# A two-layer sequence model on one core: a new order of the instructions of all engines and a new table of PSUM banks

## The chip, the cores and the metric

The kernel runs on 1 core of one Trainium2 chip. The metric is the time of the device in microseconds (us). The engines are PE (TensorE), DVE (VectorE), ACT (ScalarE), POOL (GpSimd) and SP (SyncE); each takes its own instructions strictly in the order in which the program issues them, and they meet by semaphores.

## What is computed

32 sequences of 256 positions with 128 channels go through two layers. Each layer is an adaptive-norm block: attention or a recurrence, then a feed-forward net with FP4-rounded operands. All is in float32. Cut to what matters:

```python
def layer(x, mix, ffn, c, wmod):              # c: one condition per sequence
    sa, ca, ga, sb, cb, gb = silu(c) @ wmod    # shifts, scales, gates
    x = x + ga * mix(layernorm(x) * (1 + ca) + sa)
    return x + gb * ffn(layernorm(x) * (1 + cb) + sb)

def mix0(h):     # 32 heads of 4, linear attention with 2 decays per head
    q, k = rope(h @ Wq.T), rope(h @ Wk.T); v = h @ Wv.T
    S[t] = beta[t] * S[t-1] + phi(k[t]) v[t]   # phi = elu + 1; K[t] alike
    y = sum_m mix_m * (phi(q) S_m) / (phi(q) K_m + eps)
    return layernorm(h + y @ Wout.T + bout) * g + b

def mix1(h):     # RWKV: WKV recurrence over t (max-stabilised), channel mix
    k, v, r = (shifted mixes of layernorm(h)) @ (w_key, w_value, w_recept)
    x = h + wkv(decay, first, k, v) * sigmoid(r) @ w_output
    fk, fr = (shifted mixes of layernorm(x)) @ (f_w_key, f_w_recept)
    return x + sigmoid(fr) * (relu(fk) ** 2 @ f_w_value)

def ffn(h):      # blocks of 16 are scaled by max/6 and rounded to E2M1
    q = fp4(h); t = silu(q @ fp4(w_gate).T) * (q @ fp4(w_up).T)
    return fp4(t) @ fp4(w_down).T              # 128 -> 352 -> 128
```

## The kernel before

The work is cut into 16 pairs of sequences (512 tokens, 4 tiles of 128 rows). It is a software pipeline: in turn `n` the attention step of pair `n`, the feed-forward of layer 0 of pair `n - 1`, the recurrence of layer 1 of pair `n - 2` and the feed-forward of layer 1 of pair `n - 3` run side by side. `turns` issues turns 0 to 5, then a hardware loop over turns 6 to 15 (two to an iteration), then turns 16 to 19. Turns 0 to 2 and 17 to 19 are only partly filled.

What sets the order is written out by hand, engine by engine: each engine's `body(n)` is a list of steps `do(step, pair, part)`. The eight PSUM banks are given out by the table `BANK`; a step that writes a bank first waits, with `freed` (or `freed_at_ends`, which counts only in the turns outside the loop), for the step that read it last. So a new order or a new table brings new such waits.

The names used below; the first letter tells the stage: `a` layer 0's attention, `b` a feed-forward (of layer 0 or 1), `c` layer 1's recurrence and channel mix.

- `a1n`, `a1`: ACT normalizes the rows of the input (L515), PE turns them, ACT writes `hcol` of layer 0 in two halves (L660). `a2`: PE makes keys and queries (L940), DVE multiplies by the rotary table (`rope`, L1566, keys first), `a2r` adds (L1571).
- `a4`: DVE scans (L1591) and, in `a4m`, products `state` times `rope` of 128x1024 (L1617). `a5`: the shares of the two decays, on DVE (L1624 to L1631) and PE (L1009). `a3t`: ACT halves `mixp` (L690), which `a5` needs. `a5y`: ACT copies `ycol` (L695). `a6`: PE's z-matmuls from `ycol` and `hcolb` (L1021, L1022); `a1b` makes `hcolb` on ACT (L644). `a6s`, `a6n`: squares and normalization of z on ACT (`zn`, L550, L556), between them POOL's power. `a7`: `ucol`; `a8`: rows of it to `zn` (L532), which a DMA from POOL's queue adds to x.
- `b1v`, `b1n`: squares (L525) and normalization (L515) ahead of a feed-forward, with POOL's power between them. `b1c`: the affine to `hqcol` (L660). `b1R` on PE turns it back to rows (L1063); `b1m`, `b1q` on DVE scale and round (`xblk` L1427, `hq` L1440, L1441), with ACT's `b1` (`xmag`, L712) between them. `b3`: gate and up (L1125), `th` on ACT (L708), product on DVE (L1663). `b4`, `b4q`: the same scaling and rounding of `hid`, 128x1408 (L1427, L1440, L1441), with ACT's `hidcol` (L717) between. `b5`: PE turns `hid` in two halves (L1202), ACT copies them (L724, L726), `down` multiplies (L1236); `b6g` scales by the gate (`gcol`, L660). `b6c`: the rows out, of layer 0 into `xb` (L532), of layer 1 into `drow` (L621); a DMA from POOL's queue (L466) adds `drow` to `xb`, and `store` (L882, ACT's queue) waits for it.
- `c1v`, `c1n`, `c1`: as `a1n`, `a1`, for layer 1. `c1r`, `c2s`, `c2n`, `c2`: the inner layer norm of it (L1264, L550, `norm` L556, `xs` L731), POOL's power of b1 in the middle. `c3`: three shifted products for k, v, r (L1274, L1275). `c4a`: DVE's max-scan (`epst` L1690) and `wa` (L1696); `c4`: four `relu` on ACT (L748); `c4e`: two exponentials (L753); `c4b`, `c4s`, `c4v`, `c4n`, `c4p`: DVE's part (L1702 to L1723). `c4y`: `wy`. `c5`: L1297. `c5k`: `xk` (L1738). `c6`: fk (L1330), `relu` and square on ACT (L775, L779), eight steps. `c6b`: L1338. `c7`: DVE gates it (`fth`, L1744), PE adds it up (L1102); `c9`: ACT's `acol` (L660); `c8`: rows of it to `arow` (L532), which a DMA of POOL's queue (L461) adds to `xb`.

POOL takes powers (`rstd`, L425, L416, L433) of 128x4 numbers for all norms, in one fixed circle, and issues the three adding DMAs.

## Time and profile before

| what | us |
|---|---|
| median of 3 runs | 1453.92 |
| lowest, highest | 1448.10, 1456.07 |
| the profiled execution, its own time | 1457.73 |
| its span, first to last instruction | 1454.8 |

The profile is of one execution, on the slowest (here the only) core; the 2.9 us between its time and its span lie around the span. Busy times are sums over an engine's instructions; neighbours on one engine can overlap by some tenths of a us, so the step from one start to the next can be shorter than the duration. In the timelines a bracket behind an instruction tells how long its engine had stood idle and whose work let it go. The mean clock that TensorE was granted is 0.899 of full speed.

### The profile page before, as it was taken

What the parts mean: (1) busy time and instruction counts of PE and PEld (TensorE: products, weight loads), DVE (VectorE), ACT (ScalarE), POOL (GpSimd) and SP (SyncE); (2) the same over time, 40 slices, a digit from 0 to 9 for tenths busy, and PEclk for the clock granted to TensorE, in tenths of its full rate; (3) what the DMA queues carried; (4) which work ended last, traced back from release to release, by engine and by line L of the source; (5) the groups of instructions that cost most, each with busy time, mean ns of one, the idle gap of its engine ahead of it and who ended that gap; (6) DMA issues with size and microseconds to landing.
All of it is one profiled execution on the core that took longest, in us unless ns stands there. A gap on an engine that the chain in (4) does not pass through costs nothing.

```text
span 1454.8 us, 18749 instructions
## 1 busy us (share of the span) xinstructions
PE 1157.6 (80%) x5194; PEld 706.2 (49%) x5194; DVE 1134.4 (78%) x1637; ACT 1059.1 (73%) x2849; POOL 264.5 (18%) x382
## 2 busy tenths in 40 slices
PE   5375878989797888889897988889897979878653
PEld 3133444645455554646454555546464555546332
DVE  6758595969798897969797988969797979864613
ACT  4153857779696969777796969687877969677553
POOL 1001121021212111130213122211303121211000
PEclk9676988989899999989899989999899989989776
DMA  4000000010101010100101010101001010101010
GB/s 127 0 8 8 8 15 8 9 29 1 30 8 30 8 30 9 30 7 7 29 0 30 7 29 7 30 7 22 15 7 26 4 29 8 22 8 23 0 22 15
DMA packets 28360, 25.84 MB, mean 18 GB/s; under 512 B 2304, under 2 KB 21376, under 8 KB 28288
## 3 DMA queue, kind: packets, MB, share of 16 engines
q0 software_dynamic: 6912, 12.59, 5.0%
q1 hardware_dynamic: 12928, 8.29, 1.9%
...
q14 instruction: 50, 0.41, 0.1%
...
## 4 chain that ended last, share of the span: by engine, by line
DVE 26%; PE 23%; issue 22%; ACT 20%; POOL 6%; DMA 2%; ACTq 1%; SPq 0%; DVEq 0%; POOLq 0%
PE ps L923 4%; PE ps L1236 3%; DVE hid L1440 3%; ACT hq L525 2%; PE ps L1125 2%; DVE hid L1663 2%; DVE blk L1427 2%; DVE outer L1582 2%; DVE state L1591 2%; PE ps L1202 2%; PE ps L996 2%; DVE hid L1441 2%; ACT norm L515 2%; POOL rstd_of_f L425 2%; DVE hid L1433 2%
## 5 line engine op out<-in xcount | busy, mean ns | idle before, releaser
L1125 PE MATMUL ps<-wguT,hqcol 128*128 128x352 f32 x512 | 179.8, 483 | 17.7 <-ACT th L708 7.4
L1591 DVE TENSOR_TENSOR_SCAN state<-beta,outer 128x512 f32<-128x512 f32 x128 | 148.3, 1199 | 0.0
L1125 PEld LDWEIGHTS ps<-wguT,hqcol 128*128 128x128 f32 x512 | 93.8, 197 | 86.1 <-issue 25.1
L1440 DVE SCALAR_TENSOR_TENSOR hid<-hidcol,hid 128x1408 f32<-128x1408 f32 (+1 forms) x68 | 106.4, 1569 | 11.3 <-ACT hidcol L717 10.7
L923 PE MATMUL ps<-const,hq 128*128 128x128 f32 x128 | 37.8, 386 | 88.5 <-ACT hq L515 88.4
L1427 DVE TENSOR_REDUCE xblk<-ps 128x32 f32<-128x512 f32 x32 | 22.0, 687 | 100.2 <-PE ps L1063 100.2
L1236 PE MATMUL ps<-hidcol,wdT 128*128 128x256 f32 (+1 forms) x384 | 92.6, 392 | 0.0
L1663 DVE TENSOR_TENSOR hid<-th,ps 128x352 f32<-128x352 f32 x128 | 63.1, 514 | 25.6 <-PE ps L1125 17.3
L1236 PEld LDWEIGHTS ps<-hidcol,wdT 128*128 128x128 f32 (+1 forms) x384 | 73.8, 196 | 18.7 <-issue 6.7
L996 PE MATMUL ps<-state,const 128*32 128x512 f32 x256 | 74.0, 884 | 7.2 <-DVE state L1617 7.1
L1617 DVE TENSOR_TENSOR state<-state,rope 128x1024 f32<-128x1024 f32 x64 | 75.0, 1213 | 1.7
L923 PEld LDWEIGHTS ps<-const,hq 128*128 128x128 f32 x128 | 20.4, 163 | 114.9 <-issue 67.5
L923 PE MATMUL ps<-const,norm 128*128 128x128 f32 x256 | 65.5, 341 | 12.6 <-ACT norm L515 7.0
L708 ACT ACTIVATE th<-ps 128x352 f32<-128x352 f32 x128 | 57.8, 465 | 17.7 <-DVE hid L1663 9.0
L1202 PE MATMUL ps<-const,hid 128*128 128x128 f32 (+1 forms) x384 | 52.5, 290 | 21.7 <-DVE hid L1441 21.7
L1566 DVE TENSOR_TENSOR rope<-ps,const 128x1024 f32<-128x1024 f32 x32 | 38.8, 1212 | 39.0 <-PE ps L940 39.0
L717 ACT ACTIVATE hidcol<-hid 128x1408 f32<-128x1408 f32 x32 | 44.1, 1378 | 34.0 <-DVE hid L1433 34.0
L923 PEld LDWEIGHTS ps<-const,norm 128*128 128x128 f32 x256 | 37.1, 150 | 65.3 <-issue 36.6
L465 POOL TENSOR_TENSOR pool_scrap<-minus_half,eps_tile 128x4 f32<-128x4 f32 x16 | 7.4, 465 | 335.1 <-ACT drow L621 335.1
L1690 DVE TENSOR_TENSOR_SCAN epst<-neg_w,ps 128x256 f32<-128x256 f32 x32 | 20.2, 674 | 59.7 <-PE ps L1275 59.7
L940 PE MATMUL ps<-hcol,wqk 128*128 128x512 f32 x128 | 64.2, 631 | 1.3 <-ACT hcol L660 1.3
L1330 PE MATMUL ps<-xk,fw_key 128*128 128x512 f32 x128 | 63.8, 604 | 0.0
...
## 6 DMA issues: line engine op xcount, KB each, us to landing
...
```

The costliest lines, as they stand in the source:

```text
L708: s.activation(th[l][:, t % 2, :], bank(f"f{l}_g{t}")[:, 0:I_FF], ACT.Silu).then_inc(s_th[l], 1)
L923: last = t_.transpose(dst[:, t * P:(t + 1) * P], src[:, t, :], ident)
L940: ins = t_.matmul(two_banks(("a_k", "a_q")[h])[:, n_, :], wqk[:, k, :], hcol[0][:, :], start=True, stop=True)
L996: last = t_.matmul(bank("a_n")[c * NH:(c + 1) * NH, :], cst("sel_num"), state[:, m, c, :], start=(m == 0), stop=(m == M - 1), tile_positio ...
L1125: t_.matmul(bank(f"f{l}_{'gu'[g]}{t}")[:, 0:I_FF], hqcol[l][:, t * P:(t + 1) * P], wguT[:, l, g, :], start=True, stop=True).then_inc(s_gu[ ...
L1202: last = t_.transpose(bank(f"f{l}_h{k}{'aac'[c]}")[0:rn, col:col + P], hid[l][:, 2 * k + t, r0:r0 + rn], ident)
L1236: last = t_.matmul(bank(f"f{l}_d")[:, toks], wdT[0:rn, l, c, :], hidcol[l][0:rn, c, toks], start=(c == 0), stop=(c == 2))
L1330: t_.matmul(bank(f"c_f{c}"), fw_key[:, c * P:(c + 1) * P], xk[:, :], start=True, stop=True).then_inc(s_fk_mm, 1)
L1440: return v.scalar_tensor_tensor(dst, mag, low, dst, ALU.max, (ALU.add, ALU.subtract)[part])
L1591: return v.tensor_tensor_scan(state[:, m, c, :], beta[:, m, :], src, 0.0, ALU.mult, ALU.add)
L1617: v.tensor_tensor(state[:, m, 2 * h:2 * h + 2, :], state[:, m, 2 * h:2 * h + 2, :], qshare[:, m:m + 1, :].to_broadcast([P, 2, TOK]), ALU.m ...
L1663: v.tensor_tensor(hid[l][:, t, :], th[l][:, t % 2, :], bank(f"f{l}_u{t}")[:, 0:I_FF], ALU.mult).then_inc(s_hid[l], 1)
```

## The change

All steps and their instructions stay. New are the order of the steps on ACT, PE, DVE and POOL, the table `BANK`, and the waits for free banks that follow from both. The turn is also cut at another place: what stood at the end of a turn (`a4dp`, `b4q` of layer 0, `c7` on DVE; `c6`, `b5` of layer 1, `c6b`, `c7` on PE) now opens the next turn, with `n - 1` for `n`. POOL's circle of steps is the same, cut elsewhere. In SyncE nothing changes. Line numbers behind the table are lower by one.

```diff
-BANK = {"a_b0": 5, "a_b1": 0, "a_den": 6, "a_k": 3, "a_mix": 3, "a_n": 3, "a_nT": 3, "a_q": 1, "a_s0": 3,
+BANK = {"a_b0": 3, "a_b1": 7, "a_den": 2, "a_k": 3, "a_mix": 5, "a_n": 0, "a_nT": 2, "a_q": 1, "a_s0": 4,
...
@@ POOL
-                do(power_f0, n - 2)
-                do(power_c1, n - 3)
                 do(add_x4, n - 4)
...
                 do(add_x1, n - 1)
+                do(power_f0, n - 1)
+                do(power_c1, n - 2)
@@ ACT
-                do(c9, n - 3, 0)
-                do(c9, n - 3, 1)
+                do(a3m, n - 1)
+                do(c8, n - 3)
                 do(layer(b5, 0), n - 2, 0)
                 do(layer(b5, 0), n - 2, 1)
-                do(c8, n - 3)
+                do(store, n - 4)
                 do(a3t, n - 1)
-                do(store, n - 4)
                 do(layer(b6g, 0), n - 2, 0)
                 do(layer(b6g, 0), n - 2, 1)
+                do(layer(b1v, 1), n - 3)
                 do(layer(b6c, 0), n - 2)
-                do(layer(b1v, 1), n - 3)
+                do(a1b, n - 1)
                 do(c1v, n - 2)
                 do(layer(b1n, 1), n - 3)
+                do(layer(b1c, 1), n - 3, 0)
+                do(layer(b1c, 1), n - 3, 1)
                 do(c1n, n - 2)
...
+                do(c9, n - 2, 0)
+                do(c9, n - 2, 1)
                 do(layer(b6c, 1), n - 3)
@@ PE
             def a1(i):
-                freed(pe, s_yc, i - 1)
+                freed(pe, s_xs[0], i - 2)
+                freed_at_ends(pe, s_shch, i - 1, 2, 1)
                 turn(norm[0], bank("a_nT"), "a0", i)
...
             def body(n):
+                do(c6, n - 3, 2)
+                do(b5_1, n - 4, 0)
+                do(c6, n - 3, 3)
+                do(b5_1, n - 4, 1)
+                do(b5d_1, n - 4, 0)
+                do(a3m, n - 1)
+                do(c6b, n - 3)
+                do(b5d_1, n - 4, 1)
+                do(c7, n - 3)
+                do(b6r_1, n - 4)
+                do(a4d, n - 1)
+                do(c8, n - 3)
                 do(b5_0, n - 2, 0)
                 do(b5_0, n - 2, 1)
-                do(c8, n - 3)
                 do(b5d_0, n - 2, 0)
                 do(b5d_0, n - 2, 1)
                 do(b6x_0, n - 2)
+                do(a5, n - 1, 0)
                 do(b6r_0, n - 2)
-                do(a5, n - 1, 0)
                 do(a5, n - 1, 1)
...
@@ DVE
             def body(n):
+                do(a4dp, n - 1)
+                do(layer(b4q, 0), n - 2, 0)
+                do(c7, n - 3)
+                do(layer(b4q, 0), n - 2, 1)
+                do(layer(b4q, 0), n - 2, 2)
+                do(a4, n - 1, 0, 0)
...
-                do(layer(b4q, 0), n - 1, 1)
-                do(c7, n - 2)
-                do(layer(b4q, 0), n - 1, 2)
```

Three places of the loop follow as the built programs have them; rows for semaphores and registers are left out.

ACT from `mixp` of `a3t` to the normalization `c1n` of layer 1 (`gcol` is the gated `down` of layer 0, `xb` its rows, `hq` with `squares_f` is `b1v` of layer 1). Before:

```order
L690 ACTIVATE mixp<-mixp 128x256
...
L882 DMA out<-xb 128x4x128
...
L660 ACTIVATE gcol<-ps,mod_cols 128x256
...
L532 ACTIVATE xb,sums_a<-ps 128x128 x4
...
L525 ACTIVATE hq,squares_f<-xb,negm_f 128x128 x4
L525 ACTIVATE norm,squares_a<-xb,negm_a 128x128 x4
...
L515 ACTIVATE hq<-xb,shift_of_f,rstd_of_f 128x128 x4
...
L515 ACTIVATE norm<-xb,shift_of_a,rstd_of_a 128x128 x4
```

After:

```order
L882 DMA out<-xb 128x4x128
L690 ACTIVATE mixp<-mixp 128x256
...
L660 ACTIVATE gcol<-ps,mod_cols 128x256
...
L525 ACTIVATE hq,squares_f<-xb,negm_f 128x128 x4
...
L532 ACTIVATE xb,sums_a<-ps 128x128 x4
...
L644 ACTIVATE hcolb<-hcol,bout 128x512
L525 ACTIVATE norm,squares_a<-xb,negm_a 128x128 x4
...
L515 ACTIVATE hq<-xb,shift_of_f,rstd_of_f 128x128 x4
...
L660 ACTIVATE hqcol<-ps,mod_cols 128x256
...
L515 ACTIVATE norm<-xb,shift_of_a,rstd_of_a 128x128 x4
```

The squares of `b1v` now stand ahead of the rows `xb`, `hcolb` has come in, both halves of `hqcol` stand ahead of `c1n`, and the store ahead of `mixp`.

ACT from the squares of `c2s` to the first exponential of `c4e`. Before:

```order
L550 ACTIVATE norm,squares_b<-ps 128x128 x4
...
L556 ACTIVATE norm<-ps,rstd_of_b 128x128 x4
...
L695 ACTIVATE ycol<-ps 128x512
L731 ACTIVATE xs<-ps,vec 128x2x256
...
L515 ACTIVATE norm<-xa,shift_of_a,rstd_of_a 128x128 x4
...
L550 ACTIVATE zn,squares_z<-ps 128x128 x4
...
L712 ACTIVATE xmag<-hq 128x512
...
L748 ACTIVATE ex<-wa 128x512 x2
L748 ACTIVATE ex<-wa,less 128x512
L532 ACTIVATE zn,sums_f<-ps 128x128 x4
L824 ACT_TABLE_LOAD
...
L753 ACTIVATE ex<-ex 128x2x512
```

After:

```order
L550 ACTIVATE norm,squares_b<-ps 128x128 x4
...
L695 ACTIVATE ycol<-ps 128x512
L712 ACTIVATE xmag<-hq 128x512
L556 ACTIVATE norm<-ps,rstd_of_b 128x128 x4
...
L550 ACTIVATE zn,squares_z<-ps 128x128 x4
L731 ACTIVATE xs<-ps,vec 128x2x256
...
L515 ACTIVATE norm<-xa,shift_of_a,rstd_of_a 128x128 x4
...
L748 ACTIVATE ex<-wa 128x512
L532 ACTIVATE zn,sums_f<-ps 128x128 x4
L748 ACTIVATE ex<-wa 128x512
L823 ACT_TABLE_LOAD
...
L753 ACTIVATE ex<-ex 128x2x512
```

`ycol` and `xmag` have gone ahead of the normalization by `rstd_b`; the squares of z stand ahead of `xs`, and of the four `relu` (L748) two instead of three stand ahead of the exponential.

DVE from `wa` of `c4a` to `c4v`. Before:

```order
L1696 SCALAR_TENSOR_TENSOR wa<-epst,neg_w,ps 128x512
L1440 SCALAR_TENSOR_TENSOR hq<-xmag,hq 128x512
...
L1440 SCALAR_TENSOR_TENSOR hq<-xmag,hq 128x512
...
L1441 TENSOR_TENSOR hq<-hq,xblk 128x512
...
L1566 TENSOR_TENSOR rope<-ps,const 128x1024
L1571 TENSOR_TENSOR qk<-rope 128x512
L1546 SCALAR_TENSOR_TENSOR negm_f<-sums_f,negm_a 128x4
...
L1702 TENSOR_TENSOR ex<-ex,ps 128x512
L1709 SCALAR_TENSOR_TENSOR ab<-ex 128x512
...
L1566 TENSOR_TENSOR rope<-ps,const 128x1024
...
L1709 SCALAR_TENSOR_TENSOR ab<-ex 128x512
...
L1713 TENSOR_TENSOR ex<-ex,ps 128x512
```

After:

```order
L1695 SCALAR_TENSOR_TENSOR wa<-epst,neg_w,ps 128x512
...
L1565 TENSOR_TENSOR rope<-ps,const 128x1024
L1545 SCALAR_TENSOR_TENSOR negm_f<-sums_f,negm_a 128x4
L1570 TENSOR_TENSOR qk<-rope 128x512
...
L1565 TENSOR_TENSOR rope<-ps,const 128x1024
L1570 TENSOR_TENSOR qk<-rope 128x512
...
L1701 TENSOR_TENSOR ex<-ex,ps 128x512
L1708 SCALAR_TENSOR_TENSOR ab<-ex 128x512
...
L1708 SCALAR_TENSOR_TENSOR ab<-ex 128x512
...
L1712 TENSOR_TENSOR ex<-ex,ps 128x512
```

The rounding of `hq` (`b1q` of layer 1) has gone ahead of `wa`; both `rope` products and both sums `qk` now stand ahead of `c4b` (the first `ex`), where before one product and one sum did.

## Rows read from the trace of the kernel before

**Rows 1.** Page, part 1: busy us and share of the span, by engine.

```profile
PE 1157.6 (80%) x5194; PEld 706.2 (49%) x5194; DVE 1134.4 (78%) x1637; ACT 1059.1 (73%) x2849; POOL 264.5 (18%) x382
```

**Rows 2.** Busy time by stretch: stretch, length, PE, PEld, DVE, ACT, POOL, PEclk, DMA share, GB/s.

```profile
690.70:770.90 80.20, 69.68 (x325) 42.58 (x324) 69.00 (x98) 64.33 (x177) 16.17 (x23) 0.94 0.08 17
```

**Rows 3.** Chain that ended last, in order of time: start, us, engine and line.

```profile
289.99 2.80 PE ps L1236 x12
...
450.05 2.70 PE ps L1236 x12
...
1252.71 2.80 PE ps L1236 x12
```

**Rows 4.** Timeline of DVE, one turn: start, us, instruction, [idle before <- releaser].

```profile
713.22 0.69 DVE L1427 TENSOR_REDUCE xblk<-ps 128x32 f32<-128x512 f32 x1 [4.80 <-PE ps L1063]
...
718.41 1.26 DVE L1690 TENSOR_TENSOR_SCAN epst<-neg_w,ps 128x256 f32<-128x256 f32 x2 [3.08 <-PE ps L1275]
...
724.23 1.22 DVE L1566 TENSOR_TENSOR rope<-ps,const 128x1024 f32<-128x1024 f32 x1 [1.72 <-PE ps L940]
...
726.74 0.69 DVE L1702 TENSOR_TENSOR ex<-ex,ps 128x512 f32<-128x512 f32 x1 [0.49 <-ACT ex L753]
...
737.00 0.68 DVE L1427 TENSOR_REDUCE xblk<-ps 128x32 f32<-128x512 f32 x1
737.60 1.61 DVE L1427 TENSOR_REDUCE blk<-hid 128x88 f32<-128x1408 f32 x1
...
751.59 0.74 DVE L1738 SCALAR_TENSOR_TENSOR xk<-xs,vec,xk 128x512 f32<-128x512 f32 x1
...
767.35 0.68 DVE L1744 SCALAR_TENSOR_TENSOR fth<-fth,ps 128x512 f32<-128x512 f32 x1
```

**Rows 5.** Timeline of ACT, the same turn.

```profile
696.71 0.28 ACT L532 ACTIVATE xb<-ps 128x128 f32<-128x128 f32 x1 [1.40 <-PE ps L1035]
...
698.11 0.41 ACT L525 ACTIVATE hq<-xb,negm_f 128x128 f32<-128x128 f32 x1
...
704.64 1.65 ACT L515 ACTIVATE norm<-xb,shift_of_a,rstd_of_a 128x128 f32<-128x128 f32 x4 [1.68 <-POOL shift_of_a L427]
...
713.40 0.61 ACT L695 ACTIVATE ycol<-ps 128x512 f32<-128x512 f32 x1
...
717.72 0.65 ACT L712 ACTIVATE xmag<-hq 128x512 f32<-128x512 f32 x1
...
722.41 0.71 ACT L748 ACTIVATE ex<-wa,less 128x512 f32<-128x512 f32 x1
...
725.47 1.06 ACT L753 ACTIVATE ex<-ex 128x1024 f32<-128x1024 f32 x1
...
753.21 0.71 ACT L644 ACTIVATE hcolb<-hcol,bout 128x512 f32<-128x512 f32 x1
```

**Rows 6.** Timeline of PE, the same turn.

```profile
696.46 1.14 PE L1009 MATMUL ps<-share,const 64*128 64x256 f32 x8
...
716.48 1.03 PE L1274 MATMUL ps<-xs,w_mixed 128*128 128x512 f32 x2
...
762.14 3.73 PE L1338 MATMUL ps<-fw_val,ex 128*128 128x128 f32 x32
```

**Rows 7.** Timeline of POOL, the same turn.

```profile
701.24 1.18 POOL L423 TENSOR_TENSOR var_of_a<-squares_a,eps_sum 128x4 f32<-128x4 f32 x1
702.49 1.80 POOL L425 TENSOR_TENSOR rstd_of_a<-var_of_a,minus_half 128x4 f32<-128x4 f32 x1
...
767.43 0.91 POOL L466 DMA_DIRECT2D xb<-drow  x1
```

**Rows 8.** Lines L425, L416, L466 of POOL: xcount, duration ns min/median/max, first and last start.

```profile
L425 POOL TENSOR_TENSOR rstd_of_f<-var_of_f,minus_half x32: 1032/1032/2092, 81.1 to 1404.8; 128x4 f32<-128x4 f32 x32
...
L416 POOL TENSOR_TENSOR rstd_of_a<-var_of_a,minus_half x16: 1006/1007/1032, 15.5 to 1193.4; 128x4 f32<-128x4 f32 x16
...
DMA to landing us min/median/max: 3.3/3.3/3.6
```

More of the change, by code:

```diff
@@ L805, in body @@
                 do(c1, n - 2, 1)
-                do(layer(b1c, 1), n - 3, 0)
                 do(c2s, n - 2)
-                do(layer(b1c, 1), n - 3, 1)
+                do(a5y, n - 1)
+                do(layer(b1, 1), n - 3)
                 do(c2n, n - 2)
-                do(a5y, n - 1)
+                do(a6s, n - 1)
                 do(c2, n - 2)
                 do(a1n, n)
-                do(a6s, n - 1)
+                do(a6n, n - 1)
                 do(a1, n, 0)
-                do(layer(b1, 1), n - 3)
-                do(a1, n, 1)
-                do(a6n, n - 1)
                 do(a7, n - 1, 0)
                 do(a7, n - 1, 1)
+                do(a1, n, 1)
                 do(c4, n - 2, 0)
+                do(a8, n - 1)
                 do(c4, n - 2, 1)
-                do(c4, n - 2, 2)
-                do(a8, n - 1)
                 s.preload_act_table_set("natural_log_exp_and_others")
                 do(c4e, n - 2, 0)
+                do(layer(b2, 1), n - 3)
+                do(c4, n - 2, 2)
                 do(c4, n - 2, 3)
-                do(layer(b2, 1), n - 3)
+                do(layer(b1v, 0), n - 1)
                 do(c4e, n - 2, 1)
-                do(layer(b1v, 0), n - 1)
                 s.preload_act_table_set("silu_and_others")
@@ L843, in body @@
                 do(c4l, n - 2)
+                do(a3s, n, 0)
                 do(layer(b1, 0), n - 1)
@@ L847, in body @@
                 do(c5s, n - 2)
-                do(a3s, n, 0)
+                do(layer(b4, 1), n - 3)
                 do(layer(b2, 0), n - 1)
-                do(layer(b4, 1), n - 3)
                 do(c5m, n - 2)
@@ L859, in body @@
                 do(layer(b3, 0), n - 1, 2)
-                do(a1b, n)
                 do(c6h, n - 2)
@@ L1836, in body @@
                 at_start(weight_blocks, n - 1, 1, 0, 8)
-                do(layer(b4q, 1), n - 3, 2)
-                do(a4d, n, 0)
-                at_start(weight_blocks, n, 0, 1, 6)
+                do(c5k, n - 2)
                 do(layer(b3, 0), n - 1, 2)
@@ L1843, in body @@
                 at_start(weight_blocks, n - 1, 1, 1, 1)
-                do(a3b, n, 1)
-                at_start(weight_blocks, n, 0, 1, 7)
+                do(layer(b4q, 1), n - 3, 2)
                 do(layer(b4, 0), n - 1, 0)
```

388 lines of the change are left out of this document (187 added, 201 removed), and 10 rows, old and new, of the table BANK.

## Prediction

> **What bounds the kernel now.** I read the page first: PE busy 80% of the span, DVE 78%, ACT 73% [rows 1]. No engine is full, so I asked how long one turn of the loop takes. The chain of waits meets the same piece, the twelve matmuls of `down` (L1236), again and again: at 289.99, 450.05 and 1252.71 us [rows 3]. The first two starts are two turns apart and the last two ten turns: 80.0 and 80.3 us a turn. Those 12 turns are 963 of the 1454.8 us. In one of them, DVE is busy 69.0 and PE 69.7 of 80.2 us [rows 2], so nothing is at its ceiling there: a closed loop of waits sets the turn.
>
> The DVE timeline of that turn shows where the loop runs [rows 4]. Of the rows that carry a wait, four add up to 4.80 + 3.08 + 1.72 + 0.49 = 10.09 us, all between 708 and 727. From 726.74 on DVE stands still no more until the end of `b4q` of layer 0, whose last part follows `c7` (767.35) and ends at 769.6. Half of the turn is therefore DVE work without a gap (43 us), the other half a chain of short steps on PE, ACT and POOL (37 us) from the end of `b4q` to the first exponential (`c4e`, ACT at 725.47 [rows 5]), which the DVE step `c4b` at 726.74 waits for. DVE's other work of that half lies beside the chain. A turn becomes shorter in two ways only: the chain gets shorter, or work goes from the gapless half into the 10.09 us that DVE idles. Idle time of ACT and PE outside the chain is worth nothing.
>
> **The change, part by part, for one turn of the loop.** No instruction is added or removed, so each term is a move. The tables are cut at another place of the circle (old end of turn = new start); that alone moves nothing. POOL's order is the same circle, turned: zero.
>
> *1. From `b4q` to the norm of layer 1 (`c1n`, 704.64).* On ACT the squares of `b1v` layer 1 go ahead of the rows `b6c`; they fit the 1.40 us that ACT waits before those rows [rows 5]. `a1b` (0.71 us, at 753.21 before) comes in ahead of `c1v`. On PE the first of the two `a5` (half of 1.14 us [rows 6]) now precedes the additions that the rows wait for. So the squares for a1 end 1.6 us earlier by the first move (four squares of 0.41, 0.39 start to start), and 0.6 and 0.6 later by the others: 0.4 us gained. I don't book it, because what follows on POOL may take it back (bounds: 0.6 us gained, 1.0 lost; see the rivals). `b1c` layer 1, both halves, lies in the 1.68 us that ACT waited before 704.64 [rows 5], and takes the 4.80 us gap out of DVE's middle, but it is no part of the chain. Booked: 0.
>
> *2. From `c2n` to the scans of `c4a` (718.41).* Before, ACT copied `ycol` (0.61 us) after `c2n`, then made `xs`; PE did the z-matmuls only then, and `c3` started at 716.48 [rows 6], 1.7 us after `xs` was there. Now `ycol` and `xmag` lie in POOL's `b1` wait, the z-matmuls run beside it, and what stands ahead of `xs` is `a6s` (1.1 us). `xs` is about 0.8 later, `c3` follows at once: 0.9 us gained.
>
> *3. ACT from `c2n` to the exponential (725.47).* Gone from this stretch, which had no gap but one of 0.5 us: `ycol` (0.61), `xmag` (0.65) and the third `relu` of `c4` (0.71) [rows 5]; start to start they cost 0.55, 0.52 and 0.61. With the gap that is 2.2 us. `hcol` half 1 now behind `ucol` adds a wait of 0.3 to 0.5. Gained: 1.7 us. This is the later of the two paths into `c4b`, so term 2 doesn't add to it.
>
> *4. DVE into `c4b`.* `rope` of the queries waits for PE and for `hcol`; I put it at 722.3 instead of 724.23. Now its twin and the addition `a2r` follow at once and `c4b` is behind them: 722.3 + 2 x 1.15 + 2 x 0.65 (1.22 and, for the shape of 726.74, 0.69 [rows 4]; neighbours overlap by 0.1) = 725.9. So `c4b` is 0.85 earlier than 726.74, and 1.8 us of DVE work are done that stood in the gapless half.
>
> *5. What is late next.* Not all of 0.85 + 1.8 = 2.65 stays. `c4v` waits for the second exponential, ahead of which now stand two `relu` and the squares of `b1v` layer 0; and DVE's `xblk` of layer 0 (737.00) waits for a chain over ACT (first `th`, normalization, affine, PE). These start only 0.8 and 0.25 us earlier. The reduction of `b4` layer 1 (1.61 us, 1.54 start to start [rows 4]) is put ahead of `xblk` and fills the time. At `xblk` the new order is ahead by 0.25 + 1.5 = 1.75 us. After that both orders have the same gapless 31 us up to the end of `b4q`.
>
> *6. `c7`.* It moves one part of `b4q` (1.6 us) forward, and `xk` comes later relative to it. From `xk` to `c7` DVE has 10.9 us of work by the new order. Before, the end of `xk` (751.59 + 0.74 [rows 4]) to the end of PE's L1338 (762.14 + 3.73 [rows 6]) took 13.5 us; one second half of `down` (1.4) and one half of the copies (0.85) now stand behind it, and ACT's eight steps lie closer: 10.3 to 10.9. I book 0.15 us of wait.
>
> Sum: 1.75 - 0.15 = 1.6 us a turn. It counts in the 12 turns of [rows 3] and about one more of the ramp: 13 x 1.6 = 21 us. In the last turns, where only latency counts, term 3 comes twice in part: 2 us. The first 125 us change nothing I can name. So 23 us off the profiled execution's 1457.7: 1434.7. That execution is 3.8 us above the median 1453.9; on the median's scale I say **1431**. Bounds of unknown cost alone, -1.0 and +0.6 a turn from term 1 and 0 to 0.5 from term 6: 1423 to 1448.
>
> *A rule against this change.* POOL's small operations take two lengths. The power for a1 takes 1.80 us at 702.49 while DVE scans; the same shape at L416, in a time in which DVE idles, takes 1.01; the power for f takes 1.03, and once 2.09 [rows 7, 8]. The addition at 701.24 took 1.18 and ended with DVE's product. The Trainium skill (SBUF — State Buffer, "SBUF: two separate sides") gives the reason: GpSimd and VectorE share a port pair as an exclusive lock, held for the whole instruction also by a DVE operation with two SBUF inputs. The new DVE order puts three products (`a4m`) in a row just where POOL makes a1's power. By rows alone the three steps cost 1.18 + 1.80 + 0.23 now, and 1.2 + 2.1 + 0.5 at the worst: 0.6 us more a turn, and up to 1.7 if each step waits for a whole product (1.2). It is a rival.
>
> **Rivals.**
> *More is gained.* If the squares for a1 do end earlier and POOL gets in before the products, `c1n` is 0.6 earlier and the whole chain with it, and PE's earlier `c3` and `a2` help `xblk` by some more 0.4: 2.6 a turn, 34 us in 13 turns and 2 at the end: **1418**. For it: ACT and PE have idle rows before those steps. Against: POOL's rows.
> *The head of the chain is late.* The store, which waits for the addition of `drow`, now stands ahead of `mixp` and of `gcol` on ACT. `drow` now waits behind `acol`, so behind `c7`. From POOL's start at 767.43 the transfer takes 3.3 to 3.6 [rows 8]; I put its landing at 4.3 us after `b4q`, and `gcol` at 5.1. If it lands 1 us later, or `share` does, every turn loses 0.8: 13 x 0.8 + 1 = 11 us gained only: **1443**.
> *The port takes it all.* a1's power 1.7 later: 1.6 - 1.7 = -0.1 a turn: **1453**.
> *Slower: `c7` waits.* If PE's L1338 is held up (its input needs all eight ACT steps, and a `down` of layer 1 that waits for ACT's copies stands ahead of it on PE), then two of the three parts of `b4q` are queued behind `c7` on DVE, and everyone waits for them. Before, there were 1.5 us of cover, now 0 to 0.6. Each us is one us of the turn. It decides from 1.75 us of wait; at 3 us it is 1.25 lost a turn: **1470**.
>
> **How the numbers follow.** Forecast (1423 to 1438): 0.48. More: 0.24. Late head: 0.13. Port: 0.07. `c7`: 0.08. A measurement tells about 0.5% from no change, so faster means under 1446.6, slower over 1461.2. Faster: 0.48 + 0.24 + 0.13 less a tail of 0.03 = 0.82; same 0.03 + 0.07 = 0.10; slower 0.08. The range runs from 1410 (the better case and some more in the ramp) to 1450; the port at its worst, `c7` and a still better outcome are left out.
>
> **What would show it.** The starts of L1236 78.4 to 78.8 us apart. DVE waits a turn of 10.1 down to about 8.5, the 4.80 before `xblk` of layer 1 nearly gone, one before `epst` and one before `rope` left. The wait `fth` <- PE (L1743) small; more than 1.7 us a turn there is the slow rival. POOL's three steps for a1 against 3.4 us. ACT's wait behind the store. Wrong would be a turn of 80 with the chain of waits running through POOL, or one under 77.5: then my chain holds less than I think.

## Result and the profile of the changed kernel

The changed kernel takes 1429.67 us (median of 4 runs, 1427.42 to 1434.1) against 1453.09 for the kernel before in the same session: 0.9833 of its time, 95% interval 0.9809 to 0.9858. The forecast was 1431. The profiled execution is 1434.1 us long with a span of 1432.2, 22.6 less than before.

Part 1 of its page: busy us, share of the span, instructions. It answers to [rows 1].

```profile
PE 1145.9 (80%) x5194; PEld 710.7 (50%) x5194; DVE 1135.9 (79%) x1637; ACT 1058.3 (74%) x2849; POOL 248.2 (17%) x382
```

The work is the same to 1% on PE, DVE and ACT; what went is waiting. The chain that ended last (start, us, engine and line; it answers to [rows 3]) shows how the turns changed:

```profile
285.47 2.83 PE ps L1236 x12
...
439.63 2.86 PE ps L1236 x12
...
991.43 2.83 PE ps L1236 x12
1070.31 4.50 PE ps L1236 x12
1150.21 2.83 PE ps L1236 x12
1227.01 2.83 PE ps L1236 x12
```

From 285.47 to 439.63 lie two turns written out ahead of the loop: 77.1 us each, against 80.0 of before. From 439.63 to 1227.01 lie ten: 78.7 against 80.3. So the order itself gained 2.9 us where no loop runs, more than the 1.6 booked, and about 1.4 of that went again inside the loop. There every second `down` (L1236) takes 4.1 to 4.6 us in place of 2.83: at 595.72, 753.69, 912.86 and 1070.31.

DVE from the end of `b4q` in one turn to its end in the next, with no such piece between (it answers to [rows 4]; start, us, instruction, [idle before <- releaser]):

```profile
987.08 1.62 DVE L1440 TENSOR_TENSOR hid<-hid,blk 128x1408 f32<-128x1408 f32 x1
...
996.22 0.69 DVE L1636 TENSOR_TENSOR rope<-ps,qk 128x512 f32<-128x512 f32 x1 [0.37 <-PE ps L1013]
998.37 0.69 DVE L1636 TENSOR_TENSOR rope<-ps,qk 128x512 f32<-128x512 f32 x1 [1.45 <-PE ps L1013]
...
1001.29 3.47 DVE L1616 TENSOR_TENSOR state<-state,rope 128x1024 f32<-128x1024 f32 x3
...
1008.19 0.68 DVE L1426 TENSOR_REDUCE xblk<-ps 128x32 f32<-128x512 f32 x1
...
1017.15 1.26 DVE L1689 TENSOR_TENSOR_SCAN epst<-neg_w,ps 128x256 f32<-128x256 f32 x2 [2.90 <-PE ps L1274]
...
1021.73 1.22 DVE L1565 TENSOR_TENSOR rope<-ps,const 128x1024 f32<-128x1024 f32 x1 [2.54 <-PE ps L942]
...
1025.46 0.68 DVE L1701 TENSOR_TENSOR ex<-ex,ps 128x512 f32<-128x512 f32 x1
...
1035.52 0.69 DVE L1426 TENSOR_REDUCE xblk<-ps 128x32 f32<-128x512 f32 x1
...
1062.52 0.68 DVE L1743 SCALAR_TENSOR_TENSOR fth<-fth,ps 128x512 f32<-128x512 f32 x1
...
1064.77 1.62 DVE L1440 TENSOR_TENSOR hid<-hid,blk 128x1408 f32<-128x1408 f32 x1
```

The 4.80 before `xblk` of layer 1 is gone, `c7` (1062.52) waits for nothing, and two waits of 0.37 and 1.45 us for the spread share (L1013) are new. All waits of DVE in this turn add up to 7.9 us, against 10.1. ACT in the same turn and at the next turn's start (it answers to [rows 5]):

```profile
992.61 0.42 ACT L690 ACTIVATE mixp<-mixp 128x256 f32<-128x256 f32 x1 [0.56 <-DMA xb<-drow]
994.40 0.84 ACT L660 ACTIVATE gcol<-ps,mod_cols 128x256 f32<-128x256 f32 x2 [1.38 <-PE ps L1236]
...
1003.92 1.64 ACT L515 ACTIVATE norm<-xb,shift_of_a,rstd_of_a 128x128 f32<-128x128 f32 x4
...
1023.04 1.06 ACT L753 ACTIVATE ex<-ex 128x1024 f32<-128x1024 f32 x1
...
1068.02 0.47 ACT L681 ACTIVATE mixp<-ps,bmix 128x256 f32<-128x256 f32 x1 [2.03 <-issue]
```

The last row is the piece that nobody asked for. L681 is the first step of ACT's turn in the new cut, and "issue" is time in which the engine waited for nothing that the profile shows. ACT's view of waits has it four times in the whole run, once for each jump back of the loop; PE's timeline shows what it does to `down`, and the busy times by stretch (length, busy time of each engine, PEclk, DMA share, GB/s) give the granted clock:

```profile
ACT mixp L681 <- issue: 8.4, 4, 2.2
```

```profile
1070.31 4.50 PE L1236 MATMUL ps<-hidcol,wdT 128*128 128x256 f32 x12 [2.07 <-ACT hidcol L726]
```

```profile
1070.00:1074.00 4.00, 3.69 (x11) 3.05 (x12) 3.87 (x4) 1.32 (x5) 0.62 (x1) 0.67 0.60 131
988.00:992.00 4.00, 3.11 (x25) 2.41 (x22) 4.00 (x6) 3.25 (x14) 2.37 (x4) 1.00 0.37 66
```

PE idles 2.07 us for `hidcol` and then gets a mean clock of 0.67 in place of 1.00, that is, part of the stretch at the lower of its two levels; `down` takes 4.50. In the view of waits of the kernel before, ACT has no wait for issue at all.

### The profile page after: what moved, and what is told of

Read it like the earlier page. It is cut to its first block, busy times and chain, and to the rows that moved or that the text cites. A ratio compares the mean times of both kernels' runs of the same rounds, so it can differ in the third digit from the quotient of the medians.

```text
span 1432.2 us, 18748 instructions
## 1 busy us (share of the span) xinstructions
PE 1145.9 (80%) x5194; PEld 710.7 (50%) x5194; DVE 1135.9 (79%) x1637; ACT 1058.3 (74%) x2849; POOL 248.2 (17%) x382
## 4 chain that ended last, share of the span: by engine, by line
PE 50%; DVE 17%; issue 15%; ACT 14%; DMA 3%; POOL 2%; ACTq 0%; SPq 0%; DVEq 0%; POOLq 0%
PE ps L1124 7%; PE ps L1236 6%; PE ps L1000 5%; PE ps L1337 4%; PE ps L1330 4%; PE ps L923 3%; PE ps L942 2%; DVE blk L1426 2%; ACT norm L525 2%; PE ps L1201 2%; PE ps L1273 2%; PE ps L1013 1%; DMA xa<-zn 1%; PE ps L1274 1%; PE ps L1263 1%
## 5 line engine op out<-in xcount | busy, mean ns | idle before, releaser
L1124 PE MATMUL ps<-wguT,hqcol 128*128 128x352 f32 x512 | 176.5, 480 | 21.2 <-ACT hqcol L700 19.8
L1236 PE MATMUL ps<-hidcol,wdT 128*128 128x256 f32 (+1 forms) x384 | 101.0, 410 | 16.9 <-ACT hidcol L726 16.9
L1236 PEld LDWEIGHTS ps<-hidcol,wdT 128*128 128x128 f32 (+1 forms) x384 | 74.3, 203 | 31.1 <-ACT hidcol L726 10.6
L660 ACT ACTIVATE gcol<-ps,mod_cols 128x256 f32<-128x256 f32 x64 | 26.9, 471 | 79.9 <-PE ps L1236 79.9
L1000 PE MATMUL ps<-state,const 128*32 128x512 f32 x256 | 75.8, 905 | 10.5 <-DVE state L1616 10.5
L1273 PE MATMUL ps<-xs,w_mixed 128*128 128x512 f32 x96 | 54.3, 649 | 23.7 <-ACT xs L731 23.7
L1337 PE MATMUL ps<-fw_val,ex 128*128 128x128 f32 x512 | 61.4, 278 | 1.3 <-ACT ex L779 1.3
L1201 PEld LDWEIGHTS ps<-const,hid 128*128 128x128 f32 (+1 forms) x384 | 45.6, 141 | 33.6 <-issue 29.4
L1337 PEld LDWEIGHTS ps<-fw_val,ex 128*128 128x128 f32 x512 | 58.4, 192 | 7.3 <-issue 5.0
```

The source lines that it names most:

```text
L1000: last = t_.matmul(bank("a_n")[c * NH:(c + 1) * NH, :], cst("sel_num"), state[:, m, c, :], start=(m == 0), stop=(m == M - 1), tile_positio ...
L1124: t_.matmul(bank(f"f{l}_{'gu'[g]}{t}")[:, 0:I_FF], hqcol[l][:, t * P:(t + 1) * P], wguT[:, l, g, :], start=True, stop=True).then_inc(s_gu[ ...
L1201: last = t_.transpose(bank(f"f{l}_h{k}{'aac'[c]}")[0:rn, col:col + P], hid[l][:, 2 * k + t, r0:r0 + rn], ident)
L1236: last = t_.matmul(bank(f"f{l}_d")[:, toks], wdT[0:rn, l, c, :], hidcol[l][0:rn, c, toks], start=(c == 0), stop=(c == 2))
L1273: t_.matmul(dst, w_mixed[:, k, 0, :], src[:, :, 1:T + 1], start=True, stop=False)
L1337: last = t_.matmul(bank("c_vk")[:, t * P:(t + 1) * P], fkr[:, c, t * P:(t + 1) * P], fw_val[:, c, :], start=(c == 0), stop=(c == F4 // P - 1))
```

## Experiments

All ratios are to the kernel before, on the same chip in the same session. Its medians there were 1454.1 to 1457.7 us. Differences in us between two changed kernels mostly cross sessions. Calls of `at_start`, which act for pair 0 alone, are left out of the cuts of code.

| run | what | us | ratio, 95% interval |
|---|---|---|---|
| e1_act_cut | changed; ACT's turn cut elsewhere | 1418.9 | 0.9753, 0.9732 to 0.9775 |
| e2_before_cut | before; ACT's turn cut elsewhere | 1463.6 | 1.0058, 1.0030 to 1.0086 |
| e3_dve_c | changed; second rope product back | 1452.0 | 0.9971, 0.9954 to 0.9989 |
| e8_unrolled | changed, loop written out | 1411.9 | 0.9704, 0.9680 to 0.9728 |
| e9_before_unrolled | before, loop written out | 1444.1 | 0.9908, 0.9880 to 0.9937 |
| e10_u_act_b | e8; ACT `c2n` to exponential back | 1530.4 | 1.0511, 1.0487 to 1.0535 |
| e15_u_pair | e10; PE's `a6` and `c2` back too | 1478.3 | 1.0157, 1.0133 to 1.0182 |
| e11_u_c7 | e8; `c7` back | 1434.8 | 0.9853, 0.9828 to 0.9877 |
| e16_u_c7_mix | e11; `mixp` ahead of the store | 1436.3 | 0.9864, 0.9838 to 0.9889 |
| e18_u_head | e16; PE's head of the turn back | 1472.6 | 1.0104, 1.0075 to 1.0133 |
| e13_u_c1_first | e8; `c1` ahead of one product | 1411.2 | 0.9695, 0.9672 to 0.9717 |
| e12_u_a5 | e8; both `a5` behind `b6r_0` | 1406.7 | 0.9665, 0.9640 to 0.9691 |

**Is the loss in the loop the jump of ACT's program?** Four runs move it or write it out. The first moves ACT's cut to a place where ACT waits 2.9 us for PE anyway (the first `gcol`, L660).

```diff
@@ ACT, start of body
+                do(layer(b6g, 1), n - 4, 0)
+                do(layer(b6g, 1), n - 4, 1)
+                do(c9, n - 3, 0)
+                do(c9, n - 3, 1)
+                do(layer(b6c, 1), n - 4)
                 do(a3m, n - 1)
@@ ACT, end of body
-                do(layer(b6g, 1), n - 3, 0)
...
-                do(layer(b6c, 1), n - 3)
```

> The changed kernel, with the turn of ACT's list cut at another place of the same circle: the loop's jump comes ahead of the gating of down in layer 1 (b6g), where ACT stood idle for 2.93 us, instead of ahead of mixp, where ACT has work. Theory A (the jump back of ACT's loop costs about 2.1 us each of the 4 times, and stands on the chain; PE waits behind it, its granted clock falls to 0.67 and down takes 4.5 instead of 2.8 us): the 2.1 us idle for 'issue' before mixp goes, down takes 2.8 us in every turn, two turns last 155 instead of 157.5 us, and the time falls by 10 to 14 us, to 1416 to 1420. Theory B (the time goes to the jump wherever it lies, or PE's slow stretch has another cause): nothing falls by more than 3 us.

1418.9 us, as theory A had it. ACT's wait for issue is gone from the view of waits, and all 15 `down` of the chain take 2.71 to 2.86 us. The order on the circle of steps is the same; only the place of the jump is another.

The second gives the kernel before a cut at a place where others wait for ACT.

```diff
@@ ACT of before
-                do(c9, n - 3, 0)
-                do(c9, n - 3, 1)
...
                 do(layer(b6c, 1), n - 3)
+                do(c9, n - 2, 0)
+                do(c9, n - 2, 1)
```

> The kernel before, its order unchanged, with ACT's cut moved behind acol (c9), so that the jump lies between acol and the copies of hidcol, on the chain, as in the changed kernel. Theory A: ACT idles about 2.1 us for 'issue' before hidcol in 4 turns, PE waits for it; 4 times 2 to 3.5 us, so 1461 to 1467. Theory B: 1453, no change.

1463.6 us, and the wait has appeared in the view of waits of that run:

```profile
ACT hidcol L724 <- issue: 4.0, 2, 2.0
```

The view names it at two of the four jumps. At the other two ACT stands idle for 1.94 and 1.93 us in the same place, put down to PE, where it is 0.37 in the turns between. The six runs lie in two groups, 1459 to 1460 and 1467 to 1469 us, so the cost is 5 to 14 us rather than one number; the trace is of the upper group, and its `down` behind the stop takes 2.85 us, not 4.5.

The traces hold the sequencers' own instructions too, which the views leave out.
The third and fourth write the loop out, in the new order and in the old.

```diff
-            for n in range(6):
-                body(n)
-            with eng.Fori(3, PAIRS // 2) as m:
-                body(2 * m)
-                body(2 * m + 1)
-            for n in range(PAIRS, PAIRS + 4):
+            for n in range(PAIRS + 4):
                 body(n)
```

> The changed kernel with the hardware loop written out, turns 0 to 19 in a row; the waits for free banks that are left out inside the loop are issued in every turn. Theory A: as with the moved cut, no idle 'issue' before mixp, 77.2 us in every full turn, 1415 to 1420. Theory B, that more code costs fetching from memory everywhere: 1430 or more.

1411.9 us: faster than theory A's 1415 to 1420 and than the moved cut. In its chain of waits:

```profile
668.49 2.83 PE ps L1231 x12
...
1129.31 2.83 PE ps L1231 x12
```

Six turns in 460.8 us: 76.8 each. With the moved cut the ten turns of the loop take 77.6 on average. So of the 17.8 us that writing out gains, 10.8 are the place of ACT's jump, and 7 are something else. Part of it goes over PE's clock. Both kernels have turns of two lengths: 76.2 to 77.1 us where the twelve numerator products (L995, with the loop L1000) take 3.0 to 3.2, and 77.2 to 78.2 where they take 3.8 to 3.9, partly at the lower clock. Written out, five turns of ten are short, with the moved cut three. The rest was not taken apart.

> The kernel before with its loop written out (26 turns of text in place of six, a loop of pairs and four), same order. Theory A: writing out pays in the new order alone, because there the back-jump of ACT's program falls on a step that others wait for (ACT stood still 2.2 us at it), while in the kernel before it falls where ACT waited 2.5 us for the matrix engine anyway; its turns were 80.3 us inside the loop and 80.0 outside. So 1449 to 1454 us, a gain of at most 5. Theory B: writing the loop out gains the same 18 to 21 us in any order: 1432 to 1436.

1444.1 us, between the two theories. (The text is then 20 turns long, not 26, in place of 12.) The kernel before also paid for its loop, about 1.2 us a turn (79.1 in place of 80.3 over ten turns), though none of it stands under issue on ACT, and not by ACT's jump directly: `acol`, the first step behind it, waits 2.53 us for PE in the turns with a jump and 2.44 in those without. With the loop, in one turn of a pair ACT's normalization of `hq` waited 1.32 us for POOL (0.66 without), and in the other the transposes of L1264 took 2.04 us. Written out they took 1.13 in the six middle turns of the ten, which last 78.6 to 78.8 us, and 2.05 in the other four, which last 79.7 to 79.9. What sets that off was not taken apart. Writing out gains 10.6 us in the old order and 17.8 in the new. So the new order as such is worth 32.2 us (1444.1 to 1411.9), and 23.4 of them are left with the loops.

**Is the second rope product worth its 1.8 us?** Undone alone:

```diff
@@ DVE
                 do(a2r, n, 0)
-                do(a2, n, 1)
-                do(a2r, n, 1)
                 do(c4b, n - 2)
                 do(c4s, n - 2, 0)
+                do(a2, n, 1)
                 do(c4s, n - 2, 1)
...
                 do(c4p, n - 2)
+                do(a2r, n, 1)
```

> The changed kernel with one part undone on DVE: the second rope product stands again between the two scans of ab, and its addition behind nd. By the prediction's steps 4 and 5 this part is worth 1.2 to 1.8 us a turn at c4b, of which c4v's wait for the exponential hides up to 0.6: 1.0 to 1.3 us a turn lost, 13 turns, 13 to 17 us: 1443 to 1447. The rival, that the later ACT chain hides it all: 1430.

1452.0 us: 22 of the 23.4 are lost (20 by the ratios), more than the 13 to 17 expected. DVE's timeline of that run:

```profile
1113.99 1.26 DVE L1689 TENSOR_TENSOR_SCAN epst<-neg_w,ps 128x256 f32<-128x256 f32 x2 [2.89 <-PE ps L1274]
...
1122.10 0.69 DVE L1701 TENSOR_TENSOR ex<-ex,ps 128x512 f32<-128x512 f32 x1 [1.57 <-PE ps L1274]
...
1132.18 0.52 DVE L1662 TENSOR_TENSOR hid<-th,ps 128x352 f32<-128x352 f32 x1 [0.67 <-PE ps L1124]
...
1134.59 0.69 DVE L1426 TENSOR_REDUCE xblk<-ps 128x32 f32<-128x512 f32 x1 [0.24 <-PE ps L1065]
```

`c4b` (1122.10) starts 8.1 us after the scan, where it started 8.3 after it (1017.15 to 1025.46). DVE idles 1.57 us before it instead of doing the product, does the product later, and meets two more waits for PE, 0.91 us together. From scan to `xblk` it is 20.6 us for 18.4. The mechanism of term 4 holds. Its price from scan to `xblk` is 2.2, not the 1.75 booked there; a whole turn is 1.9 longer in the loop (80.6 for 78.7) and 1.4 ahead of it (78.5 for 77.1).

**What is ACT's place from `c2n` to the exponential worth?** On the written-out kernel, undone but for `xmag`:

```diff
@@ ACT
                 do(c2s, n - 2)
-                do(a5y, n - 1)
                 do(layer(b1, 1), n - 3)
                 do(c2n, n - 2)
-                do(a6s, n - 1)
+                do(a5y, n - 1)
                 do(c2, n - 2)
                 do(a1n, n)
-                do(a6n, n - 1)
+                do(a6s, n - 1)
                 do(a1, n, 0)
+                do(a1, n, 1)
+                do(a6n, n - 1)
                 do(a7, n - 1, 0)
                 do(a7, n - 1, 1)
-                do(a1, n, 1)
                 do(c4, n - 2, 0)
-                do(a8, n - 1)
                 do(c4, n - 2, 1)
+                do(c4, n - 2, 2)
+                do(a8, n - 1)
...
                 do(layer(b2, 1), n - 3)
-                do(c4, n - 2, 2)
```

> The changed kernel with its loop written out (1411.9 us), and on ACT the stretch from the normalization of b to the exponential as it was before, all but xmag: ycol behind the normalization, the squares of z behind xs, three relu in place of two ahead of the exponential. Theory A (the prediction's terms 2 and 3: the path over xs, the scans of c4a and the exponential sets the start of c4b): the exponential is later by 0.55 + 0.52 us, of which up to 0.5 is covered by DVE, and the scans by 0.5 to 0.9: 0.5 to 1.0 us a turn, 8 to 15 us in all: 1420 to 1427. Theory B (DVE's own queue, the two rope products, sets c4b, and ACT's order there is worth nothing): 1410 to 1414.

1530.4 us, 118 more, and neither theory. Timelines of PE and ACT, and the busy times by stretch:

```profile
1085.60 0.76 PE L1018 MATMUL ps<-const,hcolb 128*128 128x128 f32 x2 [3.31 <-issue]
```

```profile
1090.24 0.78 ACT L726 ACTIVATE xs<-ps,vec 128x512 f32<-128x512 f32 x1 [4.74 <-PE ps L918]
```

```profile
1088.00:1092.00 4.00, 3.13 (x12) 2.30 (x11) 0.00 (x0) 1.76 (x4) 0.00 (x0) 0.50 0.00 0
```

In PE's new order the z-matmuls (`a6`, which need `ycol`) stand ahead of the transposes of `c2`, which `xs` needs. The bracket of 3.31 names no releaser, but `ycol` ends at 1085.49, 0.11 us before PE goes on: "issue" alone does not prove that nothing was waited for. While PE stands still the granted clock falls from 1.00 (1080 to 1084) to 0.50, the lower level (1.2 of 2.4 GHz), and what follows is slow and late: a turn takes 85.5 us for 76.8. So I undid PE's part too.

```diff
@@ PE
                 do(a4, n - 1, 1, 1)
-                do(a6, n - 1)
                 do(c2, n - 2)
+                do(a6, n - 1)
                 do(c3, n - 2, 0)
```

> The run with ACT's stretch as before had PE in the new order, where the z-matmuls (a6, which need ycol) stand ahead of the transposes of c2, on which xs waits: PE stood still for 3.31 us, its granted clock fell to 0.50 and xs waited 4.74 us. Here ACT is as in that run, and PE's a6 and c2 have their old order too (c2, then a6), so the two moves are undone together. Theory A (ACT's place and PE's place are a pair, and the 8 us a turn came from the broken pair): most of it comes back, and what is lost to the changed kernel written out (1411.9 us) is what the prediction's terms 2 and 3 booked, 0.5 to 1.4 us a turn: 1419 to 1433. Theory B (ycol behind c2n is by itself what costs, by PE's idle time and clock): 1500 to 1530.

1478.3 us: some 52 of the 118 come back, again between the theories. PE's timeline shows where the rest sits, and DVE's who pays:

```profile
1042.38 1.16 PE L918 MATMUL ps<-const,norm 128*128 128x128 f32 x4 [2.10 <-ACT norm L551]
...
1053.34 5.29 PE L937 MATMUL ps<-hcol,wqk 128*128 128x512 f32 x8
```

```profile
1056.95 1.23 DVE L1560 TENSOR_TENSOR rope<-ps,const 128x1024 f32<-128x1024 f32 x1 [6.13 <-PE ps L937]
```

With the z-matmuls behind `c2`, PE has only one numerator product left to do while POOL and ACT work on `c2n`. The kernel before kept three there (12 matmuls, 2.86 us). PE idles 2.10 us, the z-matmuls behind it take 0.63 us a pair in place of 0.39, and the queries' product L937 takes 5.29 in place of 3.66. So a third move, that of the numerator products on PE, seems to belong to the set as well; no run undid all three.

**Is `c7`'s place a cost or a gain?** The prediction booked a small cost. Undone:

```diff
@@ DVE
-                do(c7, n - 3)
                 do(layer(b4q, 0), n - 2, 1)
+                do(c7, n - 3)
                 do(layer(b4q, 0), n - 2, 2)
```

> The changed kernel with its loop written out (1411.9 us), and on DVE c7 behind two of the three parts of b4q of layer 0, as before, in place of behind one. c7 waited for nobody in the new order, so this gives DVE nothing back. Theory A: c7's place ahead is worth its 1.6 us to the store (its row goes over ACT's copy and a DMA, and ACT waited 0.56 to 0.77 us for that DMA ahead of gcol, then 1.1 to 1.4 for the matrix engine): with c7 1.6 later the store's wait grows past that, up to 0.5 us a turn lost, 1415 to 1420. Theory B: the matrix engine's down hides it: 1410 to 1414.

1434.8 us: 23 lost, 1.6 us a turn, more than theory A's price. In its timeline the share product waited 1.61 us for `mixp`, which stood behind the store. The next run takes that wait away.

```diff
@@ ACT, with c7 as in the run above
-                do(store, n - 4)
                 do(a3t, n - 1)
+                do(store, n - 4)
```

> c7 behind two parts of b4q as in the run that gave 1434.8 us, and on ACT mixp (a3t) ahead of the store again, as in the kernel before. Theory A (c7's place costs by one path alone: acol, drow, its DMA, the store that waits for it on ACT, and behind the store mixp, for which DVE's share product waited 1.61 us): the wait is gone, ACT's gcol keeps 0.3 to 1 us of it at most: 1411 to 1422. Theory B (c7's place costs by another path too, the matrix engine's acol, arow and the start of down, which began 1.6 us later after b4q in that run as well): 1428 to 1436.

1436.3 us, at the edge of theory B: the wait for `mixp` is gone and nothing is gained, so that path wasn't it. PE's timeline of this run:

```profile
1066.60 1.16 PE L1096 MATMUL ps<-const,fth 128*128 128x128 f32 x8 [1.30 <-DVE fth L1738]
1067.60 0.60 PE L1037 MATMUL ps<-const,gcol 128*128 128x128 f32 x4
1068.13 1.09 PE L985 MATMUL ps<-state,const 128*64 128x256 f32 x8
1069.15 0.66 PE L1037 MATMUL ps<-const,acol 128*128 128x128 f32 x4
1069.64 1.47 PE L1196 MATMUL ps<-const,hid 128*128 128x128 f32 x12
1071.87 2.83 PE L1231 MATMUL ps<-hidcol,wdT 128*128 128x256 f32 x12 [0.75 <-ACT hidcol L721]
```

In PE's new order three steps lie between the transposes of `c7` (L1096) and those of `hid` (L1196). A late `c7` holds up all of them, and `down` starts 3.8 us after the end of `b4q` (1068.1) in place of 2.5 with `c7` early. There `b4q` ends at 1050.6, and the row of `down` is:

```profile
1053.09 2.83 PE L1231 MATMUL ps<-hidcol,wdT 128*128 128x256 f32 x12 [0.75 <-ACT hidcol L721]
```

DVE meets the delay twice. It waits for the late `arow` ahead of `mean_f1`, which it did not with `c7` early, and then 1.00 us for the spread share of L1008 in place of 0.20:

```profile
1071.07 0.21 DVE L1552 SCALAR_TENSOR_TENSOR negm_f<-sums_f,negm_a 128x4 f32<-128x4 f32 x1 [0.42 <-issue]
```

The bracket names no releaser; ACT's `arow` ends at 1070.99.

In the kernel before the transposes of `hid` followed those of `c7` at once. If that is all, PE's old head must cure it:

```diff
@@ PE, with c7 and mixp as in the run above
-                do(c7, n - 3)
                 do(b6r_1, n - 4)
                 do(a4d, n - 1)
-                do(c8, n - 3)
+                do(c7, n - 3)
                 do(b5_0, n - 2, 0)
                 do(b5_0, n - 2, 1)
+                do(c8, n - 3)
@@ ACT
-                do(c8, n - 3)
                 do(layer(b5, 0), n - 2, 0)
                 do(layer(b5, 0), n - 2, 1)
+                do(c8, n - 3)
@@ DVE
-                do(mean_f1, n - 3)
                 do(a5, n - 1, 1)
                 do(a5, n - 1, 2)
+                do(mean_f1, n - 3)
```

> The run with c7 behind two parts of b4q and mixp ahead of the store (1436.3 us), in which PE now has the head of the turn in its old order: the transposes of c7 behind gcol's row and the decay matmuls (b6r_1, a4d), the transposes of hid (b5_0) right behind them, and acol's row (c8) last; ACT copies hidcol ahead of arow, and DVE's mean_f1 stands behind the share product, as before. Theory A (c7's early place was worth 1.6 us a turn because PE's new order puts gcol's row, the decay matmuls and acol's row, 0.60 + 1.09 + 0.66 us, between the transposes of c7 and those of hid; a late c7 then holds up down, which began 3.9 us after the end of b4q in that run, 2.6 with c7 early, and 2.0 in the kernel before with c7 late): down at 2.0 to 2.3 again, 1408 to 1420. Theory B (c7's place costs over acol and arow whatever PE's order): 1430 to 1438.

1472.6 us, worse by 36, and both theories miss. PE's timeline:

```profile
1018.58 0.60 PE L1037 MATMUL ps<-const,acol 128*128 128x128 f32 x4
1020.72 4.55 PE L1231 MATMUL ps<-hidcol,wdT 128*128 128x256 f32 x12 [1.54 <-ACT arow L527]
```

`down` now waits 1.54 us for ACT's copies of `arow`, starts 5.3 us after the end of `b4q` and takes 4.55. (Another 0.92 us pass ahead of the second half of `hid`'s transposes; no row names what for.) Behind the wait for `arow` is the other half of the change, the table of banks: it gives `acol`'s rows and `down` of layer 0 one bank (`"c_x3": 1`, `"f0_d": 1`), where the old table had 7 and 4. The code of the changed kernel says it in the step of `down`:

```
def b5d_0(i, k):
    if k == 0:
        freed(pe, s_arow, i - 1)
    ...
```

So the new table is made for an order in which `arow` is out before `down` begins. That the chain over L1096, L1196 and `down` is what `c7`'s early place shortens rests on the rows of the two runs before; this run could not confirm it, because it ran into the bank first. It is argued from timelines, not shown by a cure.

**Two moves at the head that might beat both kernels.** First `c1`'s transposes ahead of one numerator product:

```diff
@@ PE
                 do(a4, n - 1, 0, 1)
-                do(a4, n - 1, 1, 0)
                 do(c1, n - 2)
+                do(a4, n - 1, 1, 0)
                 do(b1R_1, n - 3)
```

> The changed kernel with its loop written out (1411.9 us), and on PE the transposes of c1 ahead of the third numerator product (a4 1,0) in place of behind it. In the trace of that kernel the last norm of c1n is out at 990.0 us, the transposes start at 991.1, behind twelve products of L995, and ACT waits 2.08 us for them. Theory A (this wait is on the loop that sets the turn): 0.4 to 0.9 us a turn less, 1398 to 1406. Theory B (the third product, now later, delays the numerators and with them ycol and xs by as much, or the scans of c4a wait elsewhere): 1410 to 1416.

1411.2 us, no difference to 1411.9: theory B in the time. ACT's timeline, first of the kernel without this edit, then of the one with it:

```profile
992.07 1.02 ACT L655 ACTIVATE hcol<-ps,mod_cols 128x256 f32<-128x256 f32 x2 [2.08 <-PE ps L918]
993.94 0.28 ACT L545 ACTIVATE norm<-ps 128x128 f32<-128x128 f32 x1 [0.85 <-PE ps L1258]
```

```profile
990.26 1.02 ACT L655 ACTIVATE hcol<-ps,mod_cols 128x256 f32<-128x256 f32 x2 [1.20 <-PE ps L918]
993.00 0.28 ACT L545 ACTIVATE norm<-ps 128x128 f32<-128x128 f32 x1 [1.71 <-PE ps L1258]
```

0.88 us went from the first wait and 0.86 came to the second: the product now stands ahead of the next transposes. Theory B's reason, a delay by as much further on, holds, though at an earlier step than those it named.

Then term 1's move of `a5`:

```diff
@@ PE
-                do(a5, n - 1, 0)
                 do(b6r_0, n - 2)
+                do(a5, n - 1, 0)
                 do(a5, n - 1, 1)
```

> The changed kernel with its loop written out (1411.9 us), and on PE both halves of a5 behind the additions of layer 0 (b6r_0), as before. Theory A (the prediction's term 1: the rows xb then are ready about 0.6 us sooner and the chain to c1n with them): 0.3 to 0.6 us a turn less, 1402 to 1408. Theory B (the squares for a1 wait for negm_a, and DVE reaches it only behind its second product with a5, which ends as late as before): 1409 to 1414.

1406.7 us, the fastest of all, 0.9665 of the kernel before (0.9640 to 0.9691). That is 5 us under 1411.9 from another session, and the two intervals of the ratios still overlap by 0.001. By the total theory A is right, by the reason theory B: the full turns are 76.8 us as without this edit (`down` at 742.67 and 1203.35, six turns), since the squares then wait 0.63 us for `negm_a` where they waited 0.19. The 4 us of span come from the first 743 us and from the last turns.

## Why the prediction was right, point by point

The time was right, and the mechanism (a chain of 37 us, a gapless half of 43, gains only by shortening one or by moving work out of the other into DVE's waits) stands: the chain went from 37.3 to 36.8, the other half from 42.9 to 40.9. Its terms are less right than their sum. Measured from the end of `b4q` (before: 769.6 - 80.2 = 689.4; after: 987.08 + 1.62 = 988.7), in us:

| start of | before | forecast | after |
|---|---|---|---|
| `c1n` | 15.2 | 15.2 | 15.2 |
| scans of `c4a` | 29.0 | 28.1 | 28.4 |
| exponential | 36.1 | 34.4 | 34.3 |
| `c4b` | 37.3 | 36.5 | 36.8 |
| `xblk`, layer 0 | 47.6 | 47.35 | 46.8 |
| end of `b4q` (1066.4) | 80.2 | 78.6 | 77.7 |

*Term 1* (booked 0) came out at 0, but the step behind it is another: `c1n` no longer waits for POOL, it follows `hqcol` on ACT without a gap (1003.92). The squares for a1 do not end 0.4 us earlier, they end 0.7 later (12.2 behind `b4q` for 11.5), since `down` starts 2.7 behind it for 2.1, which the term left out; POOL's steps, 0.7 shorter, make it up. *Term 2*: 0.6 of the 0.9. *Term 3* (1.7): 2.0 from `c2n` to the exponential, 1.7 at the exponential itself, as `c2n` starts 0.25 later. *Term 4*: `c4b` 0.6 earlier, not 0.85; it waits for nothing, so DVE's own queue of rope products sets it. The 1.8 us of work done beside the chain are real, as the run that undoes them shows.

*Step 5* is where the sum was wrong. I let only 0.25 us of the lead through to `xblk`, because its chain over `th` and the affine step would be late. It wasn't: `xblk` at 1035.52 has no wait, 0.8 earlier, with the reduction of `b4` (1.62 us) done before it. *Step 6*: `c7` was booked as a wait of 0.15. It waited for nothing, and its early place is no cost at all: in the written-out kernel a turn takes 1.6 us more without it (78.4 for 76.8). I looked at `c7` as a reader that might come too early, not as the producer of what PE does next. Together the turn without a jump is 2.5 us shorter in this trace (2.9 in the turns ahead of the loop), not 1.6.

What I missed on the other side is the jump: "that alone moves nothing", I wrote of the new cut. It put the start of ACT's turn where ACT has no slack and `down` waits for it. Moving only the cut gives 10.8 us back (1429.7 to 1418.9, two sessions; 0.9833 to 0.9753 as ratios). The number was thus right by luck: two errors of opposite sign, each of about 1 us a turn.

*The rivals.* The late head is there in kind (the store waits 0.56 us for its DMA at 992.61) and costs nothing: `gcol` behind it waits 1.38 more for PE. The slow case of `c7` did not happen. (The chance of 0.48 was for 1423 to 1438, while the forecast's own bounds ran to 1448, past the late head's 1443.) The port rival's price is not there. POOL's timeline, to be held against [rows 7]:

```profile
1000.98 0.39 POOL L423 TENSOR_TENSOR var_of_a<-squares_a,eps_sum 128x4 f32<-128x4 f32 x1 [2.53 <-ACT norm L525]
1001.45 1.91 POOL L425 TENSOR_TENSOR rstd_of_a<-var_of_a,minus_half 128x4 f32<-128x4 f32 x1
1003.44 0.25 POOL L427 TENSOR_TENSOR shift_of_a<-negm_a,rstd_of_a 128x4 f32<-128x4 f32 x1
```

Under DVE's three products in a row (1001.29, 3.47 us) the power takes 1.91 us, 0.11 more than before, and the addition 0.39 in place of 1.18; the three steps end 2.7 us after the first starts, against 3.4 before. The power is still some 0.9 above the 1.03 of [rows 8], so the lock that the Trainium skill describes (SBUF — State Buffer, "SBUF: two separate sides") may well be at work; nothing here shows each step waiting for a whole product.

"More is gained" (1418) has the number that the same order gives with the jump at a harmless place, but not by its mechanism: it wanted `c1n` 0.6 us earlier, and `c1n` stands where it stood.
